# Experts of four tiles packed into one 30-bit register in a two-stage mixture-of-experts kernel

## The reference

```python
x = x + _L0_xattn_ref(_layernorm(x), ...)   # attention over 1024 + new keys
x = x + _L0_ffn_ref(_layernorm(x), ...)     # 8 experts, top 2, hidden 256
x = x + _L1_xattn_ref(_layernorm(x), ...)   # attention over the context
x = x + _L1_ffn_ref(_layernorm(x), ...)     # 32 experts, top 8, hidden 192
# an expert stage, for each token t:
#   out[t] = sum over the chosen experts e of
#            weight[t, e] * ((silu(x[t] @ w_gate[e]) * (x[t] @ w_up[e])) @ w_down[e])
```

## Time and profile before

| | |
|---|---|
| median of 3 runs | 1026.26 us (1024.73 to 1031.42) |
| profiled execution | 1019.73 us, span 1017.6 us |
| busy share PE / DVE / ACT / POOL | 78% / 54% / 51% / 50% |
| first expert stage, from the first gather to the last scatter | about 284 to 404 us |
| second expert stage | about 604 to 997 us |
| tiles in both stages | 100, in 25 quads |

### The profile page before, as it was taken

The page is one execution under the profiler, slowest core; times in us unless marked ns, Lnnn a source line. Parts: engine busy times, 40 slices in busy tenths (PEclk is TensorE's granted clock), DMA queues, the critical chain, the costliest instruction groups (busy, mean ns, idle before and its releaser), DMA issues.

```text
span 1017.6 us, 19582 instructions
## 1 busy us (share of the span) xinstructions
PE 790.2 (78%) x5216; PEld 436.5 (43%) x5217; DVE 553.5 (54%) x1504; ACT 520.4 (51%) x782; POOL 507.5 (50%) x414
## 2 busy tenths in 40 slices
PE   4999999999378886575987227888878688887980
PEld 3444455554244443343434124455444355454540
DVE  5543455555636662556767324665666555455542
ACT  6532254345446663135445306676666567665750
POOL 4880000010346765200456564776777677666771
PEclk9999999999679998787998658999999899998995
DMA  8563010001166866901011035898899888888878
GB/s 282 177 207 122 3 43 32 22 22 43 28 225 163 245 137 113 324 18 42 32 43 44 25 114 148 234 241 226 209 256 242 226 223 208 207 216 220 200 136 273
DMA packets 108780, 151.89 MB, mean 149 GB/s; under 512 B 18464, under 2 KB 59680, under 8 KB 108736
## 3 DMA queue, kind: packets, MB, share of 16 engines
q1 hardware_dynamic: 80000, 93.49, 28.4%
q0 software_dynamic: 26144, 57.65, 26.7%
q10 hardware_dynamic: 2592, 0.19, 0.2%
HBM read 108.43 MB, written 42.86 MB: 149 GB/s over the span
## 4 chain that ended last, share of the span: by engine, by line
PE 41%; issue 16%; DMA 12%; DVE 11%; ACT 6%; POOL 4%; SPq 4%; another core or an unknown queue 2%; ACTq 2%; DVEq 1%; POOLq 1%; PEld 0%; PEldq 0%
PE pst L191 32%; DMA big<-in_L_ffn_w_down_dram 5%; PE pst L1276 3%; DMA x_rows<-xT,row_no 2%; POOL big L1152 2%; PE pst L506 2%; DVE big L1161 2%; ACT big L1146 1%; DMA x_rows<-mid,row_no 1%; DMA big<-x_rows 1%; POOL xT L1454 1%; PE pst L1248 1%; DVE mid L1397 1%; DMA big<-in_L_ffn_wo_dram 1%
## 5 line engine op out<-in xcount | busy, mean ns | idle before, releaser
L191 PE MATMUL pst<-big,mid 128*128 (+1 forms) x1392 | 277.2, 350 | 25.8 <-ACT mid L1312 20.6
L1012 POOL DMA_INDIRECT moe_tokens_of_experts<-token_no,small x80 | 83.1, 1039 | 290.1 <-DVE small L1065 269.7
L191 PEld LDWEIGHTS pst<-big,mid 128*128 128x128 f16 x1392 | 134.6, 100 | 133.1 <-issue 40.9
L1276 PE MATMUL pst<-big,mid 128*128 x520 | 130.7, 384 | 1.6 <-ACT mid L1323 1.0
L1312 ACT ACTIVATE mid<-pst 128x1024 f16<-128x1024 f16 x102 | 104.1, 1021 | 43.4 <-remote 27.3
L1464 POOL DMA_INDIRECT x_rows<-mid,row_no x50 | 83.9, 1678 | 42.2 <-issue 16.9
L1464 POOL DMA_INDIRECT x_rows<-xT,row_no x50 | 82.0, 1641 | 40.8 <-issue 12.3
L191 PE MATMUL pst<-ctxN,mid 128*128 128x512 f16 x384 | 91.6, 398 | 3.2 <-ACT mid L632 3.2
L1159 DVE TENSOR_TENSOR big<-big (+2 forms) x40 | 52.0, 1300 | 71.3 <-ACT big L1142 44.6
L1454 POOL DMA_INDIRECT mid<-moe_normalised_rows,row_no x56 | 61.9, 1105 | 50.2 <-DVE row_no L1372 20.9
L1389 DVE SCALAR_TENSOR_TENSOR mid<-pst,small,mid 128x192 f32<-128x192 f32 (+1 forms) x100 | 42.8, 428 | 73.4 <-ACT mid L1318 54.1
(11 more groups left out here) (214 smaller groups left out, 1308.5 us busy)
## 6 DMA issues: line engine op xcount, KB each, us to landing
big<-in_L_ffn_w_gate_dram SPq DMA_DIRECT2D x32, 384.0 KB
big<-in_L_ffn_w_up_dram SPq DMA_DIRECT2D x32, 384.0 KB
big<-in_L_ffn_wi_dram SPq DMA_DIRECT2D x16, 512.0 KB
big<-in_L_ffn_w_down_dram SPq DMA_DIRECT2D x32, 256.0 KB
big<-in_L_ffn_w_down_dram SPq DMA_DIRECT2D x64, 128.0 KB
moe_normalised_rows<-xn SPq DMA_DIRECT2D x18, 256.0 KB, 2.0
mid<-in_ctx_dram SPq DMA_DIRECT2D x16, 256.0 KB, 3.8
big<-in_ctx_turned_dram SPq DMA_DIRECT2D x16, 256.0 KB, 4.3
```

The costliest lines, as they stand in the source:

```text
L191: last = nc.tensor.matmul(dst, stationary(a, c), moving(b, c), start=(k == 0), stop=(k == 3 * len(parts) - 1))
L1012: nc.gpsimd.indirect_dma_start(out=self.tab_d[:, :], out_offset=bass.IndirectOffsetOnAxis(ap=self.addr[j % 2][:, k:k + 1], axis=0), in_=to ...
L1276: last = nc.tensor.matmul(bank(6 + p), hT[:, k, :], self.d[:, s, h, c, :], start=(q == 0), stop=(q == len(seq) - 1))
```

## The change

A new function `pack` on DVE, run once in each expert stage behind `dve_route`, makes a table `ptab` from `etab`: entry j holds the six experts j to j+5, 5 bits each. It shifts and ORs in three doublings over one partition. `experts` now loads one register, with a check of its bounds, and returns fields `(six >> 5i) & 31` of it, which become register operations where they are used. The engines wait for `tab_s` 4 in place of 3 ahead of their first load, since `pack` makes the last increment. The list of tokens (`tab`) moves to another place in the arena, since the new tables need its own.

```diff
@@ class Experts, __init__
-                self.etab = carve(mid, 10368, NE, I32)[0:1, :]
+                self.ptab = carve(mid, 10368, NE, I32)[0:1, :]
+                self.two = carve(mid, 10816, NE, I32)[0:1, :]
+                self.etab = carve(mid, 11040, NE, I32)[0:1, :]
-                self.tab = carve(mid, 10816, NT * E, I32)
+                self.tab = carve(mid, 9344, NT * E, I32)
@@ experts
-                _, values = nc.values_load_multi_w_load_instructions(
-                    self.etab[0:1, bass.ds(4 * it + first + 2, n)], engines=[eng.engine], min_val=0,
-                    max_val=self.E - 1, skip_runtime_bounds_check_because="the experts of the table are below E")
-                return values
+                six = eng.value_load(self.ptab[0:1, bass.ds(4 * it + first + 2, 1)], min_val=0, max_val=2 ** 30 - 1)
+                return [eng.snap((six >> (5 * i)) & 31).with_bounds(min_val=0, max_val=self.E - 1) for i in range(n)]
@@ quads
-                eng.wait_ge(self.tab_s, 3)
+                eng.wait_ge(self.tab_s, 4)
+            def pack(self, dve):
+                M = self.NE - 5
+                link(dve, nc.vector.tensor_scalar(self.ptab[:, 1:], self.etab[:, 1:], 5, None, ALU.logical_shift_left))
+                link(dve, nc.vector.tensor_tensor(self.two[:, 0:M + 4], self.etab[:, 0:M + 4], self.ptab[:, 1:M + 5], ALU.bitwise_or))
+                nc.vector.tensor_scalar(self.ptab[:, 0:M], self.two[:, 2:M + 2], 10, None, ALU.logical_shift_left)
+                link(dve, nc.vector.tensor_scalar(self.etab[:, 0:M], self.two[:, 4:M + 4], 20, None, ALU.logical_shift_left))
+                link(dve, nc.vector.tensor_tensor(self.ptab[:, 0:M], self.ptab[:, 0:M], self.two[:, 0:M], ALU.bitwise_or))
+                nc.vector.tensor_tensor(self.ptab[:, 0:M], self.ptab[:, 0:M], self.etab[:, 0:M], ALU.bitwise_or).then_inc(self.tab_s, 1)
@@ dve
                 self.dve_route(dve)
+                self.pack(dve)
                 self.split_d_lo(dve, 0)
```

More of the change, by code:

```diff
@@ L1351, in act @@
                 nq = self.quads(act)
-                _, e1, e2 = self.experts(act, 0, 0, 3)
+                e0, e1, e2 = self.experts(act, 0, 0, 3)
                 with act.If(e1 > 0):
@@ L1484, in pool @@
                 nq = self.quads(pool)
-                _, e1 = self.experts(pool, 0, 0, 2)
+                e0, e1 = self.experts(pool, 0, 0, 2)
                 pool.wait_ge(self.acc_in, 16 * 2 * NT)
```

## The result

The changed kernel takes 1043.34 us (median of 4 runs, 1038.33 to 1045.36) against 1028.53 (4 runs, 1024.73 to 1031.42) on the same chip: the ratio is 1.013 with a 95% interval of [1.0074, 1.0186]. It is slower by 8 to 19 us, where 1 us was forecast, and above the range of 1017 to 1038. The profiled execution has a span of 1043.7 us against 1017.6. The profiled execution is the slowest of the changed kernel's four, and that of the kernel before (1019.73 us) is faster than all four above. The ratios are those of the runs in the undisturbed state, so that the quotient of two medians of all runs can differ from them by up to 0.2%.

The account below looks back on a forecast made before the run. No single engine but a spread chain of waits was taken to bound the kernel, PE holding 41%. Pack 1.7 plus fields 3.0 less loads 4.0 gave +0.7 us on the median of 1026.26, so 1027; range 1017 to 1038.

Parts of the forecast that it names:

- The loads: Quad heads, all engines: one checked register load in place of five or six gives back 4.0 us, bounds 3.1 to 7.1.
- The fields: Register operations ahead of branches on ACT, DVE and POOL cost 3.0 us on the chain, bounds zero to 4.1.
- Rival B: Fields ahead of ACT's and DVE's branches are paid in every tile; in half of them, about 1042 us; chance 0.16.
- Pack: Six DVE instructions add 1.7 us in the first stage; in the second the wait for tokens hides them.
- Rival A: Loads at quad heads are a common barrier; shorter ones move all engines up, about 1011 to 1016 us; chance 0.12.
- Rival C: A load of one register isn't cheaper inside the loop; only checks and fields are left, 1036 us; chance 0.08.

Follow-up runs that it names:

- e1: Against the kernel before: loads of five and six experts kept on all engines, pack still runs, masks where waits use an expert; 1030.95 us, ratio 1.0052.
- e6: e1 with the packed register on PE, DVE and POOL, ACT loading five experts as before; 1031.39 us, ratio 1.0022 to the kernel before.
- e9: e1 with ACT's checked load of the expert's first tile moved from the branch to ahead of silu's wait in every tile; 993.39 us, ratio 0.9849.
- e11: e9 with the packed register on PE, DVE and POOL, ACT on its load of five; 986.58 us, ratio 0.9784 to the kernel before.
- e7: e1 with six dependent register operations ahead of each of ACT's branches; 1047.56 us, ratio 1.0177 to the kernel before.
- e3: e1 with the packed register and its fields on ACT alone; 1038.6 us, ratio 1.0139 to the kernel before.
- e8: e1 with six register operations behind each of ACT's branches, ahead of the next wait for turned rows; 1031.29 us, ratio 1.0021.

## Why the prediction was wrong

**The loads: right in direction, sized too small per load.** The new load was forecast at 0.4 to 0.55 us on POOL, PE and DVE and is 0.29 to 0.32, so packing took out more queue time than was counted. On POOL and PE the effect of the whole packed form is -6 and +3 us against e1 by the ratios, with intervals of 4 us on either side of each ratio. The sum had a gain of 4.0 us for all loads. From e1 to e6 the gain is 3 us and from e9 to e11 7 us, but both hold the cost of the fields and the lost masks of three engines as well, so they don't show the size of the loads' term by itself.

**The fields: this is the step that failed.** The prediction said "The chain passes through such a branch in 23 of the 300 places", nine of them on ACT, and charged 0.18 us for these. The cost isn't paid where the chain happens to pass. On ACT it is paid at every split, 37 times, and not in the other 63 tiles: a delay of 0.44 us ahead of each branch cost 13 us (e7), the same operations behind it nothing (e8), and taking some 0.65 us away from ahead of each split returned 21 us (e9). ACT's fields alone cost 9 us over e1 (e3), and without them the change costs nearly nothing (e6). The chain names one path through work in which tiles and weight splits run side by side.

The way from a late split to a late stage is argued and not shown. One way is the weights' cycle (DMA, ACT's split, the low parts on POOL and DVE, which free the raw buffer, the next DMA). The other is ACT itself: behind the split shown above, its second half and the next move follow without idle time, so that a late split makes ACT's next tile late too. e7, e8 and e9 fit both.

The size isn't explained in full either. The distances of the changed kernel sum to 4.8 us more than before, e3's to 5.5 us more than e1's, while 13 and 9 us were measured. In e7 and e9 the two agree better, 9.4 to 13 and 19.5 to 21. The lower clock of the changed kernel's runs (0.907 to 0.914, and 0.911 to 0.918 in e3, where the kernel before has 0.919 on average on e3's chip) may hold some of the rest.

**Rival B named the right operations but, on ACT, the wrong tiles.** It let every tile pay, and looked at L1389's waits for evidence. e8 shows that on ACT a tile without a split pays nothing; for DVE it isn't settled. Its test, waits for ACT's silu, was a test of these tiles, and so spoke against a cost that was there in the others. A row that counted was in the profile: behind the move of a result ACT was idle for about 0.5 us ahead of the split in 20 of 36 cases, and longer in most others, while its queue worked through the branch and the checked load. The profile names its own queue ("issue") for 17 of its 40 weight splits and a weight's DMA, which landed meanwhile, for 20.

**Pack** was read rightly in its place and slightly long in its size: 1.7 us were forecast in the first stage, and its six instructions put off the split behind them by 1.4. The first gather was 3.0 us later than before; the other 1.6 were there already when the tables' routing began, ahead of pack. e1, which has pack, starts it 1.5 us later than the kernel before. In the second stage DVE still waited 4.45 us for the list, of 7.13, so pack is hidden there as forecast.

**Rival A** fell. Idle time at the heads did fall by 14 us on DVE and PE together, and the changed kernel was slower all the same. **Rival C** fell with the rows of L1168 above.

**The two figures taken from the Trainium skill.** The floor of 600 ns ("DMA: Bandwidth & Descriptors", section "Latency and other measured facts") doesn't hold for these loads: all four medians are at 0.29 to 0.32 us. The 200 ns per register ("Runtime: NRT & Kernel Launch", section "Instruction fetch mechanics"; the page speaks of loads from HBM, while these read SBUF) are near the difference of the medians on DVE and POOL, (1.20 - 0.32) / 4 = 0.22, but not on ACT, (0.55 - 0.29) / 4 = 0.07, nor PE, (0.90 - 0.31) / 5 = 0.12. On POOL and DVE the loads of two registers, one at the start of each stage, support the figure: 0.52 and 0.54 us at the least, between 0.3 for one and 1.17 to 1.19 for five. The trace decides, engine by engine.

**What stays open.** That ACT's fields carry a large part of the changed kernel's 13 us is shown (9, interval about 5 on either side), and pack's 1.4 stand in its trace. Open are how a late split reaches the end of the stage, why ACT's part is more than its measured delays add up to, what the clock has to do with it, and how much of the rest DVE's branches cost and its loads give back.

## What to carry to other kernels

Look at what an engine's queue does between the last instruction and the one that others are waiting for, and price each register operation there by the turns of the loop in which that instruction runs, not by the places where the chain of waits passes. Here 0.12 us or more ahead of each of 37 weight splits outweighed 0.3 to 0.9 us of load time saved at a hundred quad heads. The remedy is one of place: on ACT the same operations behind the branch, ahead of a wait, cost nothing (e8), and a checked load of 0.5 us moved from there to ahead of a wait gave 2% (e9). To find such places, read, in order of time, the idle time ahead of an instruction that runs once per turn and on which other engines wait.

## What the runs showed of the hardware

Loads of several registers in one instruction don't cost the same on each engine: five took 0.55 us on ACT and 1.17 to 1.20 on POOL and DVE in the median, one took 0.29 to 0.32 everywhere. At the quad heads POOL's load of one register was not stretched once in 27 times (0.283 to 0.299 us), while on DVE it went up to 1.11 and on ACT to 0.80; elsewhere in the same execution a checked load of POOL took 0.67, so POOL is not free of it. And the same program is 1.6 to 1.9% faster on one chip than on two others (1008.49 against 1025.4 and 1027.85 us), more than the whole effect studied here.
